# Feed-forward part of a two-block transformer kernel: one first product moved ahead at the start of each group, and the last group finished tile by tile

## The reference

```python
x = x + _L0_xattn_ref(_layernorm(x), ctx, ctx, ...)
x = x + _L0_ffn_ref(_layernorm(x), L0_ffn_weight)
x = x + _L1_xattn_ref(_layernorm(x), ctx, ...)
x = x + _L1_ffn_ref(_layernorm(x), W1, b1, W2, b2)

# _L1_ffn_ref: EMB = 512, FF = 2048
h = einsum('bsd,fd->bsf', x, _ternary(W1)) + b1
h = gelu(h, approximate=False)
out = einsum('bsf,df->bsd', h, _ternary(W2)) + b2
```

## Time and profile before

| | |
|---|---|
| median of 3 runs | 1943.0 us (1940.11 to 1943.58) |
| profiled execution, its own time | 1943.18 us |
| its span, first to last instruction | 1941.3 us |
| TensorE busy | 90% of the span |
| VectorE, ScalarE, GpSimd busy | 64%, 54%, 47% |
| mean granted TensorE clock | 0.957 of full speed |
| feed-forward part | about 1468 us to the end |

### The profile page before, as it was taken

How to read it: one execution, slowest core, us unless ns; L and a number is a source line. 1 busy time by engine, 2 the same in 40 slices (tenths; PEclk the granted TensorE clock), 3 DMA queues, 4 the chain that set the end, 5 groups by cost and what they waited for, 6 DMA issues and landing times. The chain is left out here.

```text
span 1941.3 us, 45865 instructions
## 1 busy us (share of the span) xinstructions
PE 1745.5 (90%) x18714; PEld 1062.4 (55%) x18714; DVE 1239.1 (64%) x2454; ACT 1053.7 (54%) x1954; POOL 909.5 (47%) x1038
## 2 busy tenths in 40 slices
PE   4578899999999999999999999686659999999998
PEld 1345566666676666666666666454444444444443
DVE  4544687777877868778778687675693444344442
ACT  4546668687586686875867768453252222221221
POOL 1335457476484574754846748362351222222221
PEclk9679999999999999999999999878879999999999
DMA  5301202202112022021120220512230110111100
GB/s 171 104 28 42 80 13 80 91 2 92 40 53 91 2 91 90 2 91 40 54 91 2 91 83 11 186 51 85 71 110 33 44 44 1 44 44 44 44 22 22
DMA packets 46311, 115.56 MB, mean 60 GB/s; under 512 B 5388, under 2 KB 9612, under 8 KB 45080
## 3 DMA queue, kind: packets, MB, share of 16 engines
q1 hardware_dynamic: 43800, 104.25, 15.6%
q0 software_dynamic: 2304, 8.39, 1.1%
HBM read 72.78 MB, written 31.46 MB: 54 GB/s over the span
## 5 line engine op out<-in xcount | busy, mean ns | idle before, releaser
L751 POOL TENSOR_TENSOR arena<-arena 128x512 f16<-128x512 f32 x512 | 560.0, 1117 | 215.7 <-ACT arena L907 215.4
L899 ACT ACTIVATE arena<-psum 128x512 f32<-128x512 f32 x512 | 309.3, 611 | 107.4 <-PE psum L1436 60.8
L907 ACT ACTIVATE arena<-arena 128x512 f16<-128x512 f32 x512 | 328.0, 649 | 0.8 <-PE psum L1456 0.8
L950 ACT ACTIVATE arena<-psum,arena 128x512 f32<-128x512 f32 x128 | 88.2, 689 | 360.3 <-PE psum L1473 360.3
L1289 PE MATMUL psum<-arena 128*128 128x512 f16 x672 | 262.0, 390 | 12.0 <-DVE arena L1033 5.7
L1290 PE MATMUL psum<-arena 128*128 128x512 f16 x672 | 259.4, 386 | 0.0
L1293 PE MATMUL psum<-arena 128*128 128x512 f16 x672 | 259.1, 386 | 0.0
L1483 PE MATMUL psum<-arena 128*128 128x512 f16 x1024 | 241.9, 378 | 8.0 <-DVE arena L1226 7.2
L1473 PE MATMUL psum<-arena 128*128 128x512 f16 x1024 | 243.3, 380 | 1.4 <-DVE arena L1214 1.4
L781 POOL TENSOR_TENSOR arena<-arena 128x512 f16<-128x512 f32 x64 | 73.0, 1140 | 358.8 <-DVE arena L1221 358.8
L1221 DVE CAST arena<-arena 128x512 f16<-128x512 f32 x128 | 72.1, 563 | 255.7 <-ACT arena L950 255.7
(11 more groups left out here) (120 smaller groups left out, 3330.9 us busy)
## 6 DMA issues: line engine op xcount, KB each, us to landing
arena<-in_x SPq DMA_DIRECT2D x32, 512.0 KB, 4.5
arena<-x_scratch SPq DMA_DIRECT2D x32, 512.0 KB, 5.3
arena<-in_L_ffn_W SPq DMA_DIRECT2D x16, 1024.0 KB, 5.2
arena<-arena SPq DMA_DIRECT2D x16, 512.0 KB, 6.6
x_scratch<-arena POOLq DMA_DIRECT2D x16, 512.0 KB, 6.2
x_scratch<-arena SPq DMA_DIRECT2D x16, 512.0 KB, 3.0
out<-arena SPq DMA_DIRECT2D x16, 512.0 KB, 3.5
arena<-in_ctx SPq DMA_DIRECT2D x16, 384.0 KB, 5.3
```

The lines of the kernel that those rows point to most:

```text
L751: gp.tensor_tensor(pl[l][:, h % NP, :], pf[l][:, h % NF, :], ph[l][:, h % NP, :], ALU.subtract).then_inc(p_lo[l].sem, 1)
L899: sc.activation(pf[l][:, h % NF, :], bank(u.bank), ACT.Exp, scale=SCALE / (QS * QS) if l == 0 else SCALE).then_inc(read[u.bank], 1)
L907: sc.activation(ph[l][:, h % NP, :], pf[l][:, h % NF, :], ACT.Copy).then_inc(p_hi[l].sem, 1)
```

## The change

TensorE's `step_b` has two edits. In every group up(2) now stands ahead of down(0), not behind it. In the last group the loop does down(0) to down(13) and all first products, and leaves down(14) and down(15) to the new function `last_down`. That one goes tile by tile: for each of the 4 tiles the two matmuls of chunk 14 and the two of chunk 15, and then it raises the new semaphore `y_filled`. In `add_b` of the last group VectorE waits for `y_filled` tile by tile, and in `last_store` SP writes each tile out by itself (256 KB) when `yb_ready` says that it is added.

```diff
@@ SP
+            def last_store(s, slot):
+                for k in range(BT):
+                    sp.wait_ge(yb_ready, s * BT + k + 1)
+                    sp.dma_start(batch(od, s * GB + k // NT)[:, k % NT, :], Xb[slot][:, k, :]).then_inc(yb_stored, 16)
...
-            for s in range(B // GB):
+            for s in range(B // GB - 1):
                 store(s, s % 2)
                 if s + 2 < B // GB:
                     sp.wait_ge(yb_stored, s * (16 * GB) + 16 * GB)
                     load(s + 2, s % 2)
-            sp.wait_ge(yb_stored, 16 * B)
+            last_store(B // GB - 1, (B // GB - 1) % 2)
+            sp.wait_ge(yb_stored, 16 * (B - GB) + 16 * BT)
@@ VectorE
             def add_b(s, slot):
 
                 dve.wait_ge(xb_biased, s + 1)
-                dve.wait_ge(g_used, s * FC + FC)
+                last = s == B // GB - 1
+                if not last:
+                    dve.wait_ge(g_used, s * FC + FC)
                 for k in range(BT):
+                    if last:
+                        dve.wait_ge(y_filled, k + 1)
                     v.tensor_tensor(Xb[slot][:, k, :], bank(k), Xb[slot][:, k, :], ALU.add).then_inc(yb_ready, 1)
@@ TensorE
                 for f in range(FC):
                     if has_next and 0 <= f - TURN_AT < BT:
                         turn_b(s + 1, f - TURN_AT)
-                    down(s, f)
-                    if f + 2 < FC:
+                    if f == 0:
+                        up(s, slot, 2)
+                    if has_next or f < FC - 2:
+                        down(s, f)
+                    if 0 < f and f + 2 < FC:
                         up(s, slot, f + 2)
-                    elif has_next:
+                    elif has_next and f:
                         if f + 2 == FC:
                             pe.wait_ge(xTb_read, s * BT + 2 * BT)
                         up(s + 1, 1 - slot, f + 2 - FC)
+
+            def last_down(s):
+
+                for k in range(BT):
+                    for f in (FC - 2, FC - 1):
+                        if k == 0:
+                            g_lo_wait(pe, s, f)
+                        for n, src in enumerate((gh, gl)):
+                            mm = te.matmul(bank(k), src[:, f % NG, k * P:(k + 1) * P], w2T[:, f, :],
+                                           start=False, stop=(f + n == FC))
+                    mm.then_inc(y_filled, 1)
...
             steps_b(step_b)
+            last_down(B // GB - 1)
```

## The result

The changed kernel takes 1939.46 us (median of 17 runs, 1935.54 to 1941.98), the kernel before 1942.34 us (17 runs). The ratio is 0.9984, 95% interval 0.9977 to 0.9992: 2.9 us or 0.15% faster, between 1.6 and 4.5 us. It lies within the 0.2% that I called no change. The time is 0.1 us from the forecast of 1939.6, which is partly luck: the forecast started from about 1943.1, the level of 3 runs, where 17 runs now give 1942.34, and its gain was 3.5 us. Two differences of 0.6 to 0.8 us cancel.

A forecast was written before the change was run, and what follows sets the result against it. TensorE was taken to bound the kernel, busy 98.01 of 100 us in the feed-forward part. Terms -0.85 + 0 - 2.65 = -3.5 us, from 1943.18 or 1943.0, gave 1939.6 us; range 1937.6 to 1942.2.

The forecast's parts named there:

- Start of the first group: TensorE's wait ahead of the first down(0) is covered by up(2); gain 0.85 us.
- Later groups: At the 7 group borders down(0) has no wait to remove, so the reordering gains 0 us.
- The cause of the 7 waits: Ahead of down(15), 0.99 us each: GpSimd's bias beside VectorE's 2.90 us cast; the change moves neither.
- The end: 2.65 us: After the last group's products: 0.51 us earlier from the sums, 2.1 from the transfers, 2.65 us in all.
- The Trainium skill's price: Last store: fixed 2.0 us plus bytes / 436e3, so 2.6 us for 256 KB and total gain 3.0, not 3.5 us.
- A dear 256 KB store: Last store costs about the load's 4.2 us, or the first group's gain is lost; 1941.7 us, chance 0.2.
- The clock falling in the new wait: TensorE's last 14 matmuls run at half clock after a 1.70 us wait; 1942.6 us, chance 0.05.
- Transfers that don't overlap: Each of the four last stores begins when the one ahead has landed; about 1951.8 us at 4.2 each, chance 0.03.
- Another wait in its place: At each border another wait takes its place, so nothing is shortened; 1943 us, chance 0.06.
- a shrinking one at the borders: The 0.99 us wait ahead of down(15) shrinks at some borders; two of seven would do for 1937.6, chance 0.05.
- The sum: Whole kernel: -0.85 + 0 - 2.65 = -3.5 us, 0.18% less.

The follow-up runs named there:

- exchange alone: Kernel before with only up(2) ahead of down(0) in each group, old end kept; up(0) to the end of the span took 472.4 us.
- end alone: Changed kernel without the reordering of up(2) and down(0); from chunk 14's last product to the end of the span 8.54 us.
- stores in pairs: Changed kernel with its last group written in two 512 KB transfers; chunk 14's last product to span end 9.30 us, 0.74 longer.

## Why the prediction was right

**Start of the first group: 0.85 us.** Right without the clock: 9.50 to 8.64, in the changed kernel and with the exchange alone. In the two profiles of before and changed only 11.20 - 10.57 = 0.63 came of it, as one more matmul of the changed one ran at half clock. I had worked with the clock of one run as if it were the program's.

**Later groups: 0 us.** Right, with three readings: 6.92 us from down(15) to down(1) in both, the middle of the exchange alone within 0.1 us of before, and the same with the waits at the borders gone. In all five kernels with the bias as it was, and in before, the middle lies between 450.64 and 450.93. Most of this spread is one late reload. VectorE waits for the residual tiles of the group after, with the cast of the next chunk queued behind; in the changed kernel's profile this once held TensorE by 0.29 us (the POOL L788 row above). It is not the exchange's doing: the same place has 0.13 us of idle time in the kernel before, 0.20 with the end alone and 0.40 with stores in pairs. Without it the middle of these six is 450.51 to 450.55 us.

**The cause of the 7 waits.** The prediction put them on GpSimd's bias, from one cast of 2.90 us beside it. There it was argued; halving and moving the operation showed it. What in the chip ties the cast to the addition no run here tells.

**The end: 2.65 us.** Right: 11.19 to 8.56 is 2.63, and the end alone gives 2.65 by itself (2.72 us in both by the traces' own last instruction). Its terms: the wait grew to 1.54 us idle and the sums came at 0.86 us, so that the last sum ends 6.06 us behind chunk 14's product and not 6.62, 0.56 earlier where I had 0.51. And 256 KB landed after 2.0 us where I took 2.1.

**The Trainium skill's price.** By DMA: Bandwidth & Descriptors, section Anatomy of one DMA, the estimate for 256 KB was 2.6 us and the gain 3.0; the rows have 2.0 us, so the measurement goes against it for this store, which SP issued. The advice of that page's section Bandwidth, transfers of 1 MiB or more, is about the rate. It did not make this chain shorter: stores in pairs, 512 KB each, were 0.74 us slower. One of 1 MiB was not run.

**The rivals.** A dear 256 KB store: no, 2.0 us. The clock falling in the new wait: no, full in the 14 matmuls. Transfers that don't overlap: no, the first was issued at 1930.51 and the span ends 5.0 us later, where four in turn would need 4 x 2.0. Another wait in its place, or a shrinking one at the borders: no, VectorE's 7.0 us in 7 waits stayed.

**The sum.** Start and end together are 0.86 + 2.63 = 3.5 us in the pieces, and the runs give 2.9 (1.6 to 4.5). The two agree, and the runs can't tell more. That the time itself was met to 0.1 us is luck, as said above; the pieces are what bears the prediction out. The totals scatter for reasons that the change does not touch: within the profiles shown here, the program reached up(0) between 1464.2 and 1468.3 us, and the clock then cost 0.0 to 3.0 us more, whatever the kernel. What sets the first of these I did not look into.

## What to carry to other kernels

A gain of a few us in a program of 1940 is read by cutting the profile at fixed instructions on the bounding engine and comparing the pieces, with the granted clock taken off, and not by the span or the total. Before moving work on the bounding engine, ask which of its waits has a cause there at all: here 7 of the 8 came from one long GpSimd operation beside a VectorE cast, and cutting that operation in two gave more than twice what the change did. In a last stage, order the work so that little stands behind the last wait, and try a smaller last transfer; once the pieces come faster than they flow (0.60 against 0.70 us here), part of the gain is lost again.

## What the runs showed of the hardware

A VectorE cast from float32 to float16, 128x512 in SBUF, takes 0.43 us, but one that started well within a GpSimd addition of two SBUF tensors ended 0.3 us behind that addition at each of the three places shown: 2.90, 2.48 and 0.74 us. In the ten profiles this comes out at all 7 borders, always 0.28 to 0.29 us. GpSimd's own operation took 4.51 to 4.53 us wherever it stood. The Trainium skill, GPSIMD Engine Reference, section Key points, says that GpSimd shares its SBUF interfaces with VectorE and names contention; here it is not a slowdown of both, but the cast ends only once the addition has. As 0.28 us is less than the 0.43 us of a cast alone, either a part of it was done before or the ends in the profile are rough.

A transfer of 256 KB from SBUF to the output landed 2.0 to 2.1 us after its issue where one was issued every 0.86 us, and up to 2.3 us where one was issued every 0.60 us. One of 512 KB landed after 2.8 us.

TensorE's clock at the start of the feed-forward part differed between runs of programs that are the same up to there: the first row of matmuls ran at full clock from its beginning in two of ten profiles, and in the others between 1.7 and 3.0 us of time were lost at half clock.
